# Attention scores as float32r products on two 64-row tiles, causal mask of the exponentials on GpSimd

## The reference

```python
q_lat = (x @ Wq_down).reshape(b, t, H, L); k_lat = ...; v_lat = ...        # H=16, L=64
q = jnp.concatenate([q_c, _apply_rope(q_e, cos, sin)], axis=-1)            # [b, H, t, 16]
k = jnp.concatenate([k_c, _apply_rope(k_e, cos, sin)], axis=-1)
scores = jnp.einsum('bhqd,bhkd->bhqk', q, k) * scale
scores = jnp.where(causal[None, None], scores, -jnp.inf)
att = jax.nn.softmax(scores, axis=-1)
y = jnp.einsum('bhqk,bhkd->bhqd', att, v)                                  # then @ Wc
x = _layernorm(x + attention); x = _layernorm(x + (x + experts))
```

## Time and profile before

| | |
|---|---|
| time, median of 3 runs | 1302.01 us (1299.4 to 1308.22) |
| profiled execution | 1299.0 us, its span 1297.2 us |
| attention, with what goes with it | 0 to about 805 us |
| expert tiles and end | 805 to 1297 us |
| PE, DVE, ACT, POOL busy | 85%, 67%, 52%, 42% of the span |

### The profile page before, as it was taken

The page is one execution under the profiler, slowest core; times in us unless marked ns, Lnnn a source line. Parts: engine busy times, 40 slices in busy tenths (PEclk is TensorE's granted clock), DMA queues, the critical chain, the costliest instruction groups (busy, mean ns, idle before and its releaser), DMA issues.

```text
span 1297.2 us, 19386 instructions
## 1 busy us (share of the span) xinstructions
PE 1104.9 (85%) x6318; PEld 639.8 (49%) x6318; DVE 871.9 (67%) x2286; ACT 670.8 (52%) x1092; POOL 546.7 (42%) x405
## 2 busy tenths in 40 slices
PE   3777989899899899898988695999999998999970
PEld 1422333344343344333443231787888777877750
DVE  2466856687677678667877650667656875578886
ACT  1224655555455456545545265555566555666543
POOL 2423223222413232432231076445444467498874
PEclk9779989999899999999998697899999999999995
DMA  9535225415522552344033863011111122133336
GB/s 321 87 34 74 28 52 82 70 28 100 82 30 49 83 85 56 57 59 50 9 42 43 257 217 138 29 42 44 47 50 55 44 78 78 55 92 95 90 89 190
DMA packets 79946, 104.17 MB, mean 80 GB/s; under 512 B 12516, under 2 KB 58084, under 8 KB 79716
## 3 DMA queue, kind: packets, MB, share of 16 engines
q1 hardware_dynamic: 73704, 86.15, 31.3%
q0 software_dynamic: 6144, 16.79, 4.1%
HBM read 44.41 MB, written 33.03 MB: 60 GB/s over the span
## 4 chain that ended last, share of the span: by engine, by line
PE 44%; DVE 17%; POOL 11%; DMA 10%; SPq 8%; issue 6%; ACT 2%; POOLq 0%; ACTq 0%; DVEq 0%
PE S L778 11%; SPq L554 7%; PE O L710 6%; PE X L797 6%; PE X L675 6%; DMA W<-W 5%; DVE X L1009 5%; PE S L696 5%; POOL xs L1287 4%; DMA FA<-W 4%; DVE mx L1007 4%; POOL yn L1314 3%; POOL WL L1300 3%; PE X L733 2%; PE X L786 2%
## 5 line engine op out<-in xcount | busy, mean ns | idle before, releaser
L847 ACT ACTIVATE FA<-S 128x1024 f32<-128x1024 f32 (+3 forms) x384 | 300.0, 809 | 273.9 <-PE S L699 210.2
L1009 DVE CUSTOM_DVE_ANT_0 X<-X,MQ 128x128 f32<-128x128 f32 (+3 forms) x512 | 246.0, 505 | 128.7 <-PE X L675 126.6
L1300 POOL TENSOR_TENSOR WL<-W,WH 128x1024 fp32r<-128x1024 f32 x78 | 188.4, 2415 | 161.8 <-ACT WH L902 161.4
L1007 DVE TENSOR_REDUCE mx<-X 128x1 f32<-128x512 f32 x256 | 175.8, 687 | 34.2 <-PE X L675 34.1
L675 PE MATMUL X<-W 96*128 96x512 bf16 (+1 forms) x480 | 140.4, 341 | 47.4 <-DMA W<-W 31.3
L902 ACT CAST WH<-W 128x1024 fp32r x156 | 162.9, 1045 | 16.7 <-issue 16.2
L778 PE MATMUL S<-WH,xh 128*128 128x512 f32 x312 | 132.6, 425 | 19.6 <-POOL WL L1300 15.7
L797 PE MATMUL X<-W,hT 128*128 x624 | 147.9, 380 | 1.5 <-ACT ot L915 0.9
L696 PE MATMUL S<-W 98*128 98x512 bf16 (+1 forms) x480 | 134.1, 343 | 0.0
L1214 DVE TENSOR_TENSOR WL<-W,WH 128x1024 fp32r<-128x1024 f32 x78 | 122.9, 1576 | 2.4 <-ACT WH L902 2.2
L778 PE MATMUL S<-WH,xl 128*128 128x512 f32 x312 | 124.1, 398 | 0.0
(11 more groups left out here) (164 smaller groups left out, 1816.2 us busy)
## 6 DMA issues: line engine op xcount, KB each, us to landing
W<-W SPq DMA_DIRECT2D x120, 128.0 KB, 6.3
xs<-zt SPq DMA_DIRECT2D x78, 128.0 KB, 3.6
xg<-xs SPq DMA_DIRECT2D x78, 128.0 KB, 2.2
ys<-ot SPq DMA_DIRECT2D x78, 128.0 KB, 1.7
FA<-W SPq DMA_DIRECT2D x72, 128.0 KB, 6.1
W<-xT SPq DMA_DIRECT2D x4, 1024.0 KB, 8.5
x<-x SPq DMA_DIRECT2D x1, 4096.0 KB, 22.5
W<-wg SPq DMA_DIRECT2D x8, 512.0 KB, 10.0
```

What stands on the lines that cost most here:

```text
L847: e.activation(P[:, pr, g % 2, :, 0:w], S[pr][:, :, 0:w], ACT.Exp, scale=0.25).then_inc(act_p, 1)
L1007: t = e.tensor_reduce(mx[:, u % 2, i, 0:1], b[:, 0:w], AX, ALU.max)
L1009: t = e.tensor_tensor_reduce(b[:, 0:w], b[:, 0:w], MQ[:, 512 - w:512], 1.0, NEG, ALU.add, ALU.max, mx[:, u % 2, i, 1:2])
L1300: e.tensor_tensor(WL[:, w, :].bitcast(f32r), W[:, bass.ds(ex * WSZ, 2 * FF)], WH[:, w, :], ALU.subtract).then_inc(pool_wl, 1)
```

## The change

Queries and keys stay float32: two parts instead of three (`ph` rounded to float32r by ACT, `pl` the rest, written as float32r by POOL), and three products (high by high, high by low, low by high) instead of six. One head of a pair stands in partitions 0 to 49 and the other in 64 to 113, 48 rows of products and two rows for the maximum. A pair is now two matmuls on two 64-row tiles of the array. Projection phase 4 is gone (one ACT copy and one POOL subtraction for each half). The maxima are 24 items with two matmuls and two reductions each; a job takes two banks, and both are claimed before the first matmul. The mask matmuls of the scores are gone; instead POOL runs one `affine_select` on the exponentials of each pair in the eight diagonal steps (128 partitions, 2 x 128 elements), and `pv` of these steps waits for it. `pd` still issues twelve DMAs of 128 KB, from 32 partitions instead of 64 to 16. The maxima take four DMAs instead of two; the constant rows twelve instead of two, once. Buffers are laid out by name instead of by hand; sizes and order of the places stay about the same. The rest of the diff (names of views, waits on the renamed phases, the weights' column order) follows from these.

```diff
-MAXES = [(j, qb, k0, min((qb + 1) * 128, k0 + 512)) for j in range(4) for qb in range(8)
+MAXES = [(p, qb, k0, min((qb + 1) * 128, k0 + 512)) for p in range(2) for qb in range(8)
          for k0 in range(0, (qb + 1) * 128, 512)]
+EDGE = [n for n, (q, kb) in enumerate(STEPS) if kb >= 4 * q]
...
-        for ph in range(5):
+        for ph in range(4):
...
             add("m", u, n)
-            job("m", u, n)
-            emptied("D", "m", u, n)
-            yield (k1 - k0) / 960 + 0.07
+            for a in range(2):
+                job("m", u, n, a)
+            for a in range(2):
+                emptied("D", "m", u, n, a)
+            yield (k1 - k0) / 480 + 0.14
...
-                    q.wait_ge(pool_rope, at["E", u, 1])
-                    qo, ko = (ph, pm, ph, pm, pl, ph), (ph, ph, pm, pm, ph, pl)
-                    for sl in range(6):
+                    q.wait_ge(pool_rope, at["D", u, 1])
+                    qo, ko = (ph, ph, pl), (ph, pl, ph)
+                    for sl in range(3):
                         for which, src in ((0, qo[sl]), (1, ko[sl])):
-                            e.dma_start(KQ[s][16 * sl:16 * sl + 16, which, :, :], src[64 * which:64 * which + 64, :]).then_inc(d_kq[s], 16)
+                            for h in range(2):
+                                e.dma_start(KQ[s][64 * h + 16 * sl:64 * h + 16 * sl + 16, which, :, :],
+                                            src[64 * which + 32 * h:64 * which + 32 * h + 32, :]).then_inc(d_kq[s], 16)
...
-                    b = claim(q, "m", u, n)
+                    two = [claim(q, "m", u, n, h) for h in range(2)]
...
+                    for h, b in enumerate(two):
+                        rows = slice(64 * h, 64 * h + 48)
+                        e.matmul(b[:, 0:k1 - k0], KQ[u % 3][rows, 0, p, qb * 128:qb * 128 + 128].bitcast(f32r),
+                                 KQ[u % 3][rows, 1, p, k0:k1].bitcast(f32r),
+                                 start=True, stop=True).then_inc(pe_x, 1)
...
-                    for i in range(2):
-                        j = 2 * pr + i
-                        t = e.matmul(S[pr][:, i, 0:w], KQ[s][0:98, 1, j, kb * 128:kb * 128 + 128],
-                                     KQ[s][0:98, 0, j, qh * 512 + off:qh * 512 + 512], start=True, stop=not edge)
-                        if edge:
-                            t = e.matmul(S[pr][:, i, 0:128], identb, maskb, start=False, stop=True)
+                    for h in range(2):
+                        rows = slice(64 * h, 64 * h + 50)
+                        t = e.matmul(S[pr][:, h, 0:w], KQ[s][rows, 1, pr, kb * 128:kb * 128 + 128].bitcast(f32r),
+                                     KQ[s][rows, 0, pr, qh * 512 + off:qh * 512 + 512].bitcast(f32r), start=True, stop=True)
                     t.then_inc(pe_s, 1)
...
                     q.wait_ge(act_p, 2 * k + 2)
+                    if n in EDGE:
+                        q.wait_ge(pool_tri, 2 * (8 * u + EDGE.index(n) + 1))
...
-                    elif phase == 4:
-                        q.wait_ge(act_part, at["m", u, ch])
-                        e.tensor_tensor(pl[:, cs], t1[:, ch, :], pm[:, cs], ALU.subtract).then_inc(pool_rope, 1)
+                        e.tensor_tensor(pl[:, cs].bitcast(f32r), t1[:, ch, :], ph[:, cs], ALU.subtract).then_inc(pool_rope, 1)
+                elif kind == "s":
+                    u, n, pr = a
+                    if n in EDGE:
+                        g = 12 * u + n
+                        q.wait_ge(act_p, 2 * g + pr + 1)
+                        e.affine_select(P[:, pr, g % 2, :, 0:128], P[:, pr, g % 2, :, 0:128], pattern=[[0, 2], [1, 128]],
+                                        compare_op=ALU.is_ge, fill=zero, base=0, channel_multiplier=-1).then_inc(pool_tri, 1)
```

More of the change, by code:

```diff
@@ new lines, in program @@
+        with ExitStack() as before:
+            WD0, WD1 = (sb(f"WD{i}", [128, 8, C], c=before) for i in range(2))
+        KQ1 = kq_("KQ1")
+        XT1 = xt_("XT1")
+        RP = sb("RP", [128, 2, T], c=att)
+        WE = sb("WE", [128, 2, 3 * C + E], c=att)
+        tr, tq, t1 = (sb(n, [128, 2, 512], c=att) for n in ("tr", "tq", "t1"))
+        ph, pl = (sb(n, [128, T], c=att) for n in ("ph", "pl"))
+        with ExitStack() as before:
+            WD2 = sb("WD2", [128, 8, C], c=before)
+        KQ2 = kq_("KQ2")
@@ L1338 @@
     rope[9::2, 1] = sin[1::2]
-    rope = c(np.tile(np.repeat(rope, 4, 0), (2, 1, 1)))
+    rope = c(np.tile(np.repeat(rope, 2, 0), (4, 1, 1)))
     x = a["L0_attn_x"].reshape(N, C)
```

145 lines of the change are left out of this document (66 added, 79 removed).

## The result

The changed kernel takes 1462.38 us (median of 4, 1460.38 to 1474.79) where the kernel before takes 1301.96: a ratio of 1.124, 95% interval 1.118 to 1.130. Forecast were 1334 us and a range from 1294 to 1358. Slower was right; the loss is 160 us, not 32.

A forecast was written before the change was run, and what follows sets the result against it. The loop was taken as bound by 15.9 us of DMA plus about 29.5 us of mostly DVE work, the end by POOL's scatter queue. Terms -7 + 4 - 1 + 36 = +32 us gave 1334 us, range 1294 to 1358.

The forecast's parts named there:

- The loop: Thirteen attention stretches: DVE's waits -20, claim +6, selects +4, clock +3, so -7 us; unit 0, like a plain stretch, -1.
- The saving on PE: Scores and maxima in each attention unit: paired row tiles relieve PE of about 6.5 us a unit.
- DVE: Attention loop: DVE's unchanged work bounds what PE's saving yields; its waits for PE shrink 20 us, bounds 0 and 41.
- The claim: Maxima: two of three banks per pair cost +6 us in the loop, +5 in the first maxima (bounds 0 and 8).
- Before unit 0: Start of attention: phase 4 removed -2.3, two more DMAs +1.2, claim in first maxima +5, together +4 us.
- The selects: Mask on POOL: 0.7 us each, delaying `pv` in narrow diagonal steps, +4 us in the loop (bounds 0 and 20).
- The end: End of attention: selects of units 14 and 15 queue among and behind POOL's 48 scatters, 98.6 us against 62.2, +36.
- The transfers: DMAs between units: same count and bytes, issue to landing stays 15.9 us; an estimated 0.9 us gain left out.
- (a): Loop: DVE's waits for PE vanish altogether, -41 instead of -20, without the claim's costs: 1302 us; chance 0.16.
- (b): Loop follows PE: transfers start earlier and each of 14 units loses 6.5 us: 1250 us; chance 0.07.
- (c): Transfers: alternating partition halves run side by side, group 11 us instead of 15.7, -66 in 14 units: 1268 us; chance 0.07.
- (d): Scores and maxima: row tiles do not overlap, a pair costs 0.48 us and PE is not relieved: 1362 us; chance 0.13.

The follow-up runs named there:

- late_mask_pe: Changed kernel with the mask back on PE and the second bank of a pair claimed late: ratio 1.074, 51.2 us a unit.
- mask_pe: Changed kernel with the mask put back on PE as identity times mask products, nothing on POOL: ratio 1.100, 53.7 us a unit.
- claim_late: Changed kernel, but PE waits for the second bank of a pair of maxima only right before the second product: ratio 1.056.
- after: The changed kernel itself, against the kernel before: 1462.38 us, ratio 1.124, 53.0 us a unit.
- after_again: The changed kernel run once more, nothing altered: ratio 1.122 to the kernel before, 52.6 us a unit.
- mask_pool: Kernel before with the mask part alone: no mask products on PE, affine_select on POOL instead, bf16 limbs kept: ratio 1.028.
- late_bf16: Changed kernel with the second bank of a pair claimed late and scores and maxima read as bf16: ratio 1.028, 48.2 us a unit.
- max64: Kernel before with the contraction of its maxima cut from 96 rows to 64: 1455 us in a single run.
- max66: Kernel before with the contraction of its maxima cut from 96 rows to 66: 1379.62 us in a single run.
- max48: Kernel before with only the contraction of its maxima cut from 96 rows to 48: 1448.82 us, ratio 1.065.
- no_select: Changed kernel with the causal mask left out, so no affine_select on POOL and no wait for one: 1462 us, ratio 1.085.
- filler: Changed kernel with an added bf16 product of 128 rows, later overwritten, ahead of each pair of scores: ratio 1.202, 60.7 us a unit.

## Why the prediction failed, step by step

**The loop (forecast -7 and -1, measured +108).** This is the step that failed: its term for the clock and the tiles. I had put +3 us for it, from stretches with 0.92, 0.93 and 1.00; I took a low clock as what follows a wait for the landing. In the kernel before such a place can be found. Here is its stretch with the wait, then the one after it:

```profile
252.40:259.20 6.80, 1.54 (x14) 0.48 (x10) 1.21 (x1) 1.66 (x3) 2.33 (x2) 0.91 1.08 161
259.20:266.00 6.80, 6.80 (x48) 2.63 (x47) 3.52 (x12) 2.08 (x5) 2.53 (x2) 0.58 0.21 74
```

The changed kernel has long stretches at 1.2 GHz with PE at work in them:

```profile
249.00:272.80 23.80, 19.94 (x104) 8.89 (x105) 15.75 (x49) 10.22 (x15) 9.20 (x15) 0.50 0.11 38
```

I had counted the rows of a product as free, and nothing in the trace of before said otherwise, as all its products of scores and maxima are of the one kind. By the runs, 107.9 us in 13 units split into about 6.5 a unit, 85 in all, for float32r on row tiles with its clock (late_mask_pe), 2.4 for the claim (mask_pe against late_mask_pe; 1.7 by claim_late), and -0.7 to -1.1 for the mask going from PE to POOL (after and after_again against mask_pe). Each is a difference of single executions and good to about 1 us.

The saving on PE, 6.5 us for each unit in the forecast (its own terms, 10 and 8 down to 5.5 each, give 7), was mis-sized as well. At full clock 1.2 us of it can be seen, in the twelfth unit of claim_late against mask_pool. The sum priced a product by the distance between two float32r matmuls and left its weight load at what the bf16 limbs had; the load took 232 ns instead of some 100.

**DVE (forecast: DVE bounds the loop).** I had DVE's waits for PE shrink by 20 us. They grew by 77: from 109.9 and 30.2 us ahead of the two reductions in the units to 147.6 and 69.4. These groups of DVE show it, first in the kernel before, then in the changed one (count, busy us, mean ns, idle before and its releaser). The claim has a part in it: in claim_late the two are 155.6 and 37.9 us, so 53 of the 77 remain.

```profile
L1009 DVE CUSTOM_DVE_ANT_0 X<-X,MQ 128x512 f32<-128x512 f32 (+3 forms) x417 | 200.6, 506 | 111.5 <-PE X L675 109.9
L1007 DVE TENSOR_REDUCE mx<-X 128x1 f32<-128x512 f32 x208 | 142.9, 687 | 30.2 <-PE X L675 30.2
```


```profile
L1017 DVE CUSTOM_DVE_ANT_0 X<-X,MQ 128x512 f32<-128x512 f32 (+3 forms) x417 | 197.6, 516 | 148.8 <-PE X L689 147.6
L1015 DVE TENSOR_REDUCE mx<-X 128x1 f32<-128x512 f32 x208 | 133.8, 685 | 70.1 <-PE X L689 69.4
```

**The claim (forecast +5 before unit 0, +6 in the loop).** The mechanism was right, the size was not: 9.4 us before the first `mm`, above my bound of 8, and some 22 to 32 us in the loop, within the bound of 0.3 us for each of 15 pairs. The first maxima of the changed kernel, where the earlier trace rows has 23.89 of 24.20 us busy on DVE:

```profile
51.90:87.20 35.30, 16.50 (x48) 7.59 (x48) 26.38 (x80) 1.24 (x2) 4.02 (x4) 0.50 0.34 45
```

**Before unit 0 (forecast +4, measured +11.7).** The claim's error is 4.4 us of the 7.7. The rest lies in what I had put at -1.1 without it: claim_late reaches its first `mm` at 77.8, 2.3 us after the kernel before. late_bf16 gets there at 76.1, so 1.7 us of that go with the type; the remaining 1.7 us no run explains.

**The selects (forecast 0.7 us each, +4 in the loop).** They took 0.41, and `pv` waited for them; the answer on line 1287 of the changed kernel has ns min/median/max, then who waited (us, times):

```profile
L1287 POOL TENSOR_SCALAR_AFFINE_SELECT P<-P x256: 399/407/424, 94.5 to 964.5; 128x256 f32<-128x256 f32 x128
...
  PEld O L722: 47.4, 33
  PE O L722: 40.9, 18
```

Of the 47.4 and 40.9 us, 29.5 and 26.5 lie behind the first scatter. For the loop, the two executions without selects have units 0.9 us shorter on average than the two with them, 12 us over thirteen: above the +4 and inside its bounds, but no larger than what one kernel varies by. In mask_pool the thirteen units are as long as before, though PE has 32 mask products less in each.

**The end (forecast +36, measured +42).** The mechanism is in the trace as forecast. The rows are the first scatter, a select between two scatters, the last scatter with the last three selects of unit 14 behind it, the last selects of unit 15, and SP's first fetch:

```profile
875.94 1.20 POOL L1301 DMA_INDIRECT xs<-x,posi  x1 [3.37 <-DVE posi L1201]
...
880.96 0.42 POOL L1287 TENSOR_SCALAR_AFFINE_SELECT P<-P 128x256 f32<-128x256 f32 x1
881.55 0.98 POOL L1301 DMA_INDIRECT xs<-x,posi  x1 [0.17 <-issue]
...
938.47 0.96 POOL L1301 DMA_INDIRECT xs<-x,posi  x1 [0.30 <-issue]
939.44 1.12 POOL L1287 TENSOR_SCALAR_AFFINE_SELECT P<-P 128x256 f32<-128x256 f32 x3
...
963.22 1.70 POOL L1287 TENSOR_SCALAR_AFFINE_SELECT P<-P 128x256 f32<-128x256 f32 x4 [0.72 <-ACT P L856]
```

```profile
966.96 3.72 SPq L608 DMA_DIRECT2D xg<-xs  x5
```

From first scatter to fetch it is 91.0 us against the 98.6 of the sum. The scatters with the nine selects between them took 63.5 us, and with the three behind them 64.6, not 69.7, for a select of 0.41 us uses up part of a pause of 0.3 that POOL made anyway; from there to the fetch it is 26.4 us for the 28.9 of the sum. That is +29, below the lower bound of 31 by 2 us. The other 13.6 of the 42.4 us lie ahead of the first scatter, in a stretch with a clock of 0.56 where the kernel before has 0.78. So the total of the end came out near the forecast partly by luck: its own term was 7 us too high, and the clock, which the sum did not have there, made up for it. mask_pool has +32 for both together.

**The transfers (taken as unchanged).** They landed a little earlier: median and longest over the line are below, 6.3 and 9.0 in the earlier trace rows.

```profile
DMA to landing us min/median/max: 3.2/5.4/7.6
```

At the median that is 14% less. The Trainium skill, page "SBUF — State Buffer", section "Can I just issue two DMAs to hit both halves?", has two transfers at partitions 0 and 64 only 6% faster. The measured gain is larger, but the transfers differ in shape as well as in place, and no run took the places alone. It was worth little, for PE was late by then: it waited 7.4 us in all for line 564, where the kernel before waited 48.1 us for its line 554. The forecast had this wait grow.

**The rivals.** (a) and (b) are out: the waits of DVE grew, and the unit of the changed kernel is longer, not below 40 us; the 6.5 us that (b) has each unit save is not reached even in the twelfth unit of claim_late. (c) and (d) are out: landings are about 1 us shorter, not 4.7, and the tiles overlap. The case that came true, row tiles that cost PE its clock, was not among them. The cost at each change of tile shape, which I had put at an estimated 1 us a stretch and left within the range, is a candidate for 2.0 us a unit at full clock (max64 against max66), and it doesn't eat up the saving by itself: late_bf16 changes shape at the same places and has 37.8 us for the twelfth unit at a clock of 1.00, where mask_pool has 39.4.

## What to carry to other kernels

Look at the granted clock of a kernel before cutting the rows of its products, and measure one cheap edit of the rows alone, as max48 does. This kernel stood at 0.95 with its PE on 128-row products, and 64-row ones cost it more than the shorter product saved, with nothing in the profile of before to announce it. A claim of two buffers of three takes away the double buffering (here 1.7 to 2.4 us a unit); claim each at its use. Work that is put on a queue with a long burst of other work in it (here 48 scatters) must be costed at that burst, not at its own length.

## What was not expected of the hardware

- The clock of the kernel before depends on two rows: 66 rows in the maxima give 0.91 and 46.7 us a unit, 64 rows give 0.84 and 52.2.
- Added full-array work lifts the clock in one case and not in another: mask products of 128 rows brought 0.75 (no_select) to 0.79 (mask_pe); the filler left it at 0.74, where it is 0.74 and 0.75 without, and a filler of dense data had 0.72.
- An affine_select of 128 x 256 float32 on POOL takes 0.41 us, a third less than the 0.60 us of the tensor_scalar of as many elements in the earlier trace rows.
- Some chips give this kernel 50 us more in one place, the last unit's maxima, and next to none elsewhere. The cause stays open.
